# Two self attentions fused with the projection and layer norm ahead of them, and a first expert whose rows are picked by a one-hot product, in a two-layer perceiver block

## What is computed

```python
x = x + L0_xattn(layernorm(x), ctx)   # cross attention, projection+norm, self attention, projection+norm, MLP
x = x + L0_attn(layernorm(x))
x = x + L0_ffn(layernorm(x))          # 32 experts
x = x + L1_xattn(layernorm(x), ctx)   # cross attention, projection
x = x + L1_attn(layernorm(x))         # causal self attention, 16 heads of 16
x = x + L1_ffn(layernorm(x))          # 8 experts, below
# L1_ffn: each expert takes its 65 best tokens of each batch
scores = softmax(x @ router_w.T); gate, idx = top_k(scores.T, 65)
h = gelu(x[idx] @ w1 + b1); y = (h @ w2 + b2) * gate; out[idx] += y
```

## Time and profile before

| what | us |
|---|---|
| three timed runs, median (lowest to highest) | 1703.92 (1701.82 to 1704.51) |
| the profiled execution, its own time | 1701.66 |
| its span, first to last instruction | 1699.4 |
| TensorE busy | 1609.7 (95%) |
| VectorE busy | 1138.1 (67%) |
| ScalarE busy | 862.2 (51%) |
| GpSimd busy | 286.4 (17%) |
| layer 0: projection, norm and self attention | 660.9 to 732.3 |
| layer 1: projection, norm and causal self attention | 1519.7 to 1586.1 |
| last experts | 1598.1 to 1699.4 |

### The profile page before, as it was taken

One profiled execution on the slowest core, in us unless ns is written; L12 is line 12 of the kernel. 1 busy time (PEld: TensorE's weight loads), 2 busy tenths in 40 slices (PEclk: granted clock), 3 DMA queues, 4 the chain that ended last, 5 costly groups with the idle time before them and its releaser, 6 DMA issues. The chain is left out here.

```text
span 1699.4 us, 36130 instructions
## 1 busy us (share of the span) xinstructions
PE 1609.7 (95%) x12499; PEld 972.8 (57%) x12499; DVE 1138.1 (67%) x2012; ACT 862.2 (51%) x1784; POOL 286.4 (17%) x372
## 2 busy tenths in 40 slices
PE   7999999999999998999989999889999999989697
PEld 4444444454544544675867999635445454445497
DVE  5777788888888884747553111288888888855621
ACT  2222216777777775642532111257777777765332
POOL 1422220000000001020202444130000000000063
PEclk9999999999999999999989999989999999999899
DMA  6568756434434324400038999754343443304075
GB/s 194 180 201 219 205 165 137 75 57 65 65 56 69 60 38 127 67 2 1 1 112 274 325 314 320 238 85 66 57 74 56 66 64 56 56 1 102 13 220 141
DMA packets 150585, 196.29 MB, mean 116 GB/s; under 512 B 30394, under 2 KB 123805, under 8 KB 144465
## 3 DMA queue, kind: packets, MB, share of 16 engines
q1 hardware_dynamic: 141704, 188.83, 45.3%
q0 software_dynamic: 6720, 4.31, 1.5%
q10 hardware_dynamic: 2064, 1.87, 0.3%
HBM read 156.49 MB, written 41.39 MB: 116 GB/s over the span
## 5 line engine op out<-in xcount | busy, mean ns | idle before, releaser
L1187 ACT ACTIVATE probs<-ps 128x512 f32<-128x512 f32 x1024 | 558.5, 599 | 179.1 <-PE ps L1090 166.6
L1213 DVE TENSOR_REDUCE top<-ps 128x1 f32<-128x1024 f32 x504 | 594.1, 1220 | 60.1 <-PE ps L1069 47.1
L1090 PE MATMUL ps<-qst,kst 105*128 105x256 bf16 x2048 | 354.2, 276 | 6.8 <-DVE qst L1218 1.5
L1069 PE MATMUL ps<-kst,qst 105*128 105x512 bf16 x1008 | 306.3, 387 | 5.2 <-DVE top L1213 3.6
L1090 PEld LDWEIGHTS ps<-qst,kst 105*128 105x128 bf16 x2048 | 170.3, 100 | 227.5 <-ACT probs L1187 86.3
L1104 PE MATMUL ps_o<-probs,vst 128*32 128x256 f32 x4096 | 274.1, 385 | 2.3 <-ACT probs L1187 2.3
L1104 PEld LDWEIGHTS ps_o<-probs,vst 128*32 128x32 f32 x4096 | 106.8, 109 | 113.4 <-issue 50.9
L383 POOL COPY vst<-vall 128x512 f32 (+1 forms) x64 | 39.2, 613 | 697.0 <-PE ps_o L1104 694.3
L2312 PE MATMUL ps_h<-xe,vall 128*128 128x80 f32 x1024 | 149.6, 265 | 0.0
L2312 PEld LDWEIGHTS ps_h<-xe,vall 128*128 128x128 f32 x1024 | 136.4, 191 | 0.1
L1069 PEld LDWEIGHTS ps<-kst,qst 105*128 105x128 bf16 x1008 | 88.7, 98 | 62.9 <-issue 29.2
(11 more groups left out here) (439 smaller groups left out, 2008.8 us busy)
## 6 DMA issues: line engine op xcount, KB each, us to landing
kst<-kd SPq DMA_DIRECT2D x372, 128.0 KB
kd<-probs SPq DMA_DIRECT2D x64, 384.0 KB, 2.8
vall<-in_L_ffn_wg_dram SPq DMA_DIRECT2D x32, 512.0 KB, 6.3
vall<-in_L_ffn_wu_dram SPq DMA_DIRECT2D x32, 512.0 KB, 7.9
vall<-in_L_ffn_wd_dram SPq DMA_DIRECT2D x32, 512.0 KB, 5.9
w<-in_L_ffn_w_dram SPq DMA_DIRECT2D x16, 1024.0 KB, 7.4
vd<-square_weights SPq DMA_DIRECT2D x16, 512.0 KB, 4.1
vall<-vd SPq DMA_DIRECT2D x16, 512.0 KB, 6.3
```

The lines of the kernel that those rows point to most:

```text
L1069: mm = pe.matmul(ps1[:, slot1(m, u), x * 512:(x + 1) * 512], qst[:, m, qt * P:(qt + 1) * P], kst[:, m, c * W1 + x * 512:c * W1 + (x + 1) * ...
L1090: mm = pe.matmul(ps2[:, SCORES2[u], x, :], kst[:, m, kt * P:(kt + 1) * P], qst[:, m, :], start=True, stop=True)
L1187: nc.scalar.activation(probs[:, u % SLOTS, :, :], ps2[:, SCORES2[u], :, :], ACT.Exp).then_inc(probs_ready, 1)
L1213: v.tensor_reduce(top[:, b, qt, c:c + 1], ps1[:, slot1(m, u), :], AX, ALU.max).then_inc(mx, 1)
```

## The change

`normalize_and_attend` takes the place of `project_and_normalize` and `self_attention` where one followed the other (twice). It is one block: keys and queries of group 0 are made, copied and used by batch. The norm block behind the causal attention stays as it was. SyncE issues both sets of loads at the start of the fused block. In `experts1` the first expert's rows are picked from `xn` in SBUF by a product with a one-hot matrix, `first_hot`; gathers are left for the experts 1 to 7. The second part of the tables and the biases are moved into `up(0)`, the biases to other PSUM banks, the wait for the base ahead of `down(0)`, `turn_x(1)` behind `down(0)`. There are 45 filler matmuls in four places instead of 16 in one, and Gelu's table is loaded early. The core of the diff:

```diff
-def self_attention(pr, xT, query, key, value, causal, ahead=lambda sp: None):
+def normalize_and_attend(pr, src_tile, K, weight, bias, residual, total, query, key, value, causal, gain=None, shift=None,
+                         ahead=lambda sp: None, ahead_of_units=lambda sp: None):
...
+    FIRST_OF = {0: 1, 2: 2, 8: 3}
...
                 ahead(sp)
 
+                ahead_of_units(sp)
...
-                keys(0)
-                queries(0)
+                turn_src(0)
+                turn_src(1)
+                stay_busy(ps_f, 3)
+                for t in range(NT):
+                    project(t)
+                    if t + 2 < NT:
+                        turn_src(t + 2)
+                for t in range(QT):
+                    stay_busy(ps_t[:, 0, :], 3)
+                    turn_normed(t)
+                stay_busy(ps_t[:, 0, :], 2)
+                pe.wait_ge(x_copied, 1)
+                keys(0, 0, S)
+                queries(0, 0, S)
+                for t in range(QT, NT):
+                    turn_normed(t)
+                stay_busy(ps_p[:, 2, :], 2)
                 scores(0)
+                pe.wait_ge(x_copied, 2)
+                keys(0, S, N)
+                queries(0, S, N)
                 scores(1)
                 values()
                 keys(1)
...
-                copy_k(0)
+                copy_k(0, 0, slice(0, S))
+                copy_x(1)
                 exps(0, 0)
                 exps(0, 1)
-                copy_k(1)
+                copy_k(0, 1, slice(S, N))
+                copy_k(1, 2)
...
-                copy_q(0)
+                copy_q(0, 0, slice(0, S))
                 maxima(0)
+                copy_q(0, 1, slice(S, N))
                 maxima(1)
                 copy_v()
-                copy_q(1)
+                copy_q(1, 2)
...
-                for e in range(XB1):
+                pool.wait_ge(slots_ready, 1)
+                for e in range(1, XB1):
...
+                def first_x():
+                    pe.wait_ge(first_ready, 1)
+                    for b in range(B):
+                        for c in range(C):
+                            for t in range(b * QT, (b + 1) * QT):
+                                mm = pe.matmul(ps_x[:, c, b * CAP:(b + 1) * CAP], xn[:, t, c * P:(c + 1) * P],
+                                               first_hot[:, t, :], start=(t == b * QT), stop=(t == b * QT + QT - 1))
+                    mm.then_inc(x_turned, 1)
...
                 mm.then_inc(sc_t, 1)
+                stay_busy(38)
                 pe.wait_ge(taken_ready, 1)
...
                 mm.then_inc(taken_t, 1)
+                stay_busy(2)
                 pe.wait_ge(chosen_ready, 1)
...
                 mm.then_inc(placed, 1)
+                stay_busy(3)
+                first_x()
                 table(0)
...
+                stay_busy_in(ps_h[:, NH - 1, :], 2)
                 for e in range(E1):
                     for f in range(FT1):
                         up(e, f)
-                        if f == TURN_Y_AT and e:
-                            turn_y(e - 1)
-                        if f == TURN_X_AT and e + 1 < E1:
-                            turn_x(e + 1)
+                        if e == 0:
+                            if f == TABLE_AT:
+                                table(1)
+                            if f == BIAS_AT:
+                                bias()
+                        else:
+                            if f == TURN_Y_AT:
+                                turn_y(e - 1)
+                            if f == TURN_X_AT and e + 1 < E1:
+                                turn_x(e + 1)
                     down(e)
+                    if e == 0:
+                        turn_x(1)
...
+                nc.scalar.activation(first_gelu[:, :], pr.cf("parity")[:, 0:1], ACT.Gelu)
                 copy_x(0)
...
+                v.tensor_tensor(first_hot[:, :, :], bc(pr.cf("iota")[:, 1:CAP + 1], 1, NT), bc(slot[:, :, 0], 2, CAP),
+                                ALU.is_equal).then_inc(first_ready, 1)
...
-                v.tensor_tensor(base[:, :, :], acc, residual[:, :, :], ALU.add).then_inc(base_ready, 1)
+                v.tensor_tensor(base[:, 0:QT, :], ps_b[:, :, :], residual[:, 0:QT, :], ALU.add)
+                v.tensor_tensor(base[:, QT:NT, :], ps_y_rows, residual[:, QT:NT, :], ALU.add).then_inc(base_ready, 1)
```

More of the change, by code:

```diff
@@ L1316, in self_attention @@
             "summed", "o_copied", "o_turned", "inverted", "o_done"))
+        srcT = pr.sb(st, "srcT", [P, NT, K * P])
+        added = residual if bias is None else pr.sb(st, "added", [P, NT, D])
+        centred = pr.sb(st, "centred", [P, NT, D])
+        stats = pr.sb(st, "stats", [P, NT, 6])
+        mv = pr.sb(st, "mv", [P, NT, 2])
+        std = pr.sb(st, "std", [P, NT])
+        rstd = pr.sb(st, "rstd", [P, NT])
+        first_root = pr.sb(st, "first_root", [P, 1])
+        ps_p = ps_s.rearrange("p n j k -> p (n j) k")
+        ps_x = ps_of.rearrange("p x (c n) -> p x c n", c=C)
+        src_turned, copied, made, bias_added, steps, var_ready, std_ready, done, x_turned = (pr.sem(st, n) for n in (
+            "src_turned", "copied", "made", "bias_added", "steps", "var_ready", "std_ready", "done", "x_turned"))
+        x_copied = pr.sem(st, "x_copied")
         with nc.Block() as block:
@@ L1330, in _, with turn_src, project, stay_busy @@
             def _(pe):
[L1331 removed]
+                def turn_src(t):
+                    if t >= 2:
+                        pe.wait_ge(copied, t - 1)
+                    for c in range(K):
+                        mm = pe.transpose(ps_t[:, t % 2, c * P:(c + 1) * P], src_tile(t, c), pr.cf("ident"))
+                    mm.then_inc(src_turned, 1)
+                def project(t):
+                    pe.wait_ge(copied, t + 1)
+                    for c in range(K):
+                        mm = pe.matmul(ps_p[:, t, 0:D], srcT[:, t, c * P:(c + 1) * P], weight[:, c, :],
+                                       start=(c == 0), stop=(c == K - 1))
+                    mm.then_inc(made, 1)
+                def stay_busy(bank, n):
+                    for _ in range(n):
+                        pe.matmul(bank, pr.cb("identb"), pr.constsb[:, 0:512], start=True, stop=True)
+                def turn_normed(t):
+                    pe.wait_ge(done, t + 1)
+                    for c in range(C):
+                        mm = pe.transpose(ps_x[:, t // 2, c, (t % 2) * P:(t % 2 + 1) * P], dst[:, t, c * P:(c + 1) * P],
+                                          pr.cf("ident"))
+                    mm.then_inc(x_turned, 1)
+                def keys(c, first=0, end=N):
                     for x in range(C):
[L1333 removed]
+                        mm = pe.matmul(ps_kq[c][0][:, first:end], wk[:, x, c * P:(c + 1) * P], xT[:, x, first:end],
                                        start=(x == 0), stop=(x == C - 1))
                     mm.then_inc(k_made, 1)
[L1337 removed]
+                def queries(c, first=0, end=N):
                     for x in range(C):
[L1339 removed]
+                        mm = pe.matmul(ps_kq[c][1][:, first:end], wq[:, x, c * P:(c + 1) * P], xT[:, x, first:end],
                                        start=(x == 0), stop=(x == C - 1))
```

144 lines of the change are left out of this document (98 added, 46 removed).

## The result

The changed kernel takes 1696.17 us in the median of seven runs (1695.65 to 1699.26), the kernel before 1703.92 in seven (1701.82 to 1705.72). The ratio is 0.996, 95% interval 0.9951 to 0.997. The medians differ by 7.75 us; the ratio alone makes it 6.8 (5.1 to 8.3). The forecast was 1695.3 (1692.0 to 1699.5), faster with a chance of 0.89. The profiled execution of the changed kernel took 1695.69 us with a span of 1693.7. That is 5.97 less than the profiled execution before, where the sum of the prediction was 8.6.

The account below looks back on a forecast made before the run. TensorE, busy 95% of the span, was taken as the bound, so gains lie where it waits or runs at 1.2 GHz. 2.8 + 3.4 + 2.4 = 8.6 us off 1703.92 gave 1695.3 (own range 1692.6 to 1698.2).

Parts of the forecast that it names:

- Layer 0: First fused attention: first turn of the loop at 685.8 instead of 688.66, saving 2.8 us (2.8 to 4.0).
- Layer 1: Second fused attention: first turn of the loop at 1542.8 instead of 1546.25, saving 3.4 us.
- Cost nothing: Fused blocks: GpSimd's clearing of the value tile and SyncE's loads, moved along, add no time.
- The sign that it gave: Stage behind a fused block: waits behind the moved loads would show as TensorE idle at its start; none expected.
- The last block: Marks to second expert: early first `up`, partly given back, second expert at 1628.9 instead of 1631.32; saves 2.4 us (1.4 to 3.3).
- `down(0)` 3.58: Last block: the first expert's down product takes 3.58 us, ending at 1628.0.
- the gap ahead of `down(0)`: Last block: TensorE waits near 0.9 us for VectorE to add the base.
- Checked and not binding: Last block: second one-hot ready by 1620.3, expert 1's gathers have until 1628, expert 2's weights in time; no cost.
- From expert 1 on the cadence is TensorE's: Last block: from expert 1 on TensorE sets the pace as before, and the tail is the same.
- B: Rival, both fused blocks: ScalarE 1.4 us later behind the table load, by a drain; costs 2.2 us, 1697.5; 6%.
- C: Rival: stretches shorter, but new waits or 1.2 GHz elsewhere leave half; saving 3.6 to 5, 1699 to 1700.3; 18%.
- E: Rival, last block: the 38 fillers don't raise the clock; 9.2 us slower, 1713.1; 4%.

Follow-up runs that it names:

- e1: Changed kernel with the last expert block (`experts1`) of before, so both fused attentions alone: 1698.13 us, ratio 0.9969 to the kernel before.
- e6: Changed kernel with 33 instead of 38 fillers ahead of the marks' transposes: 1696.89 us, ratio 0.9929 to the kernel before.
- e12: Changed kernel without the early Gelu on ScalarE, so Gelu's table is loaded again behind the first expert's row copy: 1697.18 us, ratio 0.9965.
- e2: Kernel before with the new `experts1`, norm and attention blocks as before: 1702.14 us, ratio 0.9993 to the kernel before.
- e4: Changed kernel with biases behind table(0) in place of two fillers, and the base added ahead of the second table's slots: 1695.06 us, ratio 0.9952.
- e5: Changed kernel with five filler matmuls on TensorE ahead of `down(0)`: 1696.65 us, ratio 0.9933 to the kernel before.
- e8: e4 with 33 fillers instead of 38: 1695.07 us, ratio 0.9918 to the kernel before.
- e9: e4 with three experts in the first table instead of two: 1694.01 us, ratio 0.9944 to the kernel before.
- e11: e9 with GpSimd's wait for the base's store moved behind the gather of expert 4: 1693.78 us, ratio 0.995.

## Why the prediction was right or wrong

**The number** was right: 1696.17 against 1695.3, inside the range. The attentions did what the prediction said; in the last block the 2.4 of the sum were 0.1. That the number came so near in spite of this is in part luck. In the first pair of profiles the steps that were changed save 1.98 + 3.22 + 0.1 = 5.3 us, which would have given 1698.6, outside the forecast's own range to 1698.2. The other 2.4 of the 7.75 come from none of these steps. A part may be the stretch at 1.2 GHz that the old block of layer 1 shows in two of three profiles, 1.1 on the mean; the rest has no place that the traces show.

**Layer 0: right up to the first turn.** 2.8 forecast, 2.62 measured, in all ten profiles of the fused block by batch. TensorE's order came as worked out, and the scores cost all of the 1.16 that the bounds allowed. The path is 0.24 longer than forecast, 15.15 instead of 14.91: 0.18 stands ahead of the scores of pair 1, mostly keys and queries of batch 1, 1.93 instead of 1.75. ScalarE's second key copy wasn't the limit; it ended 7.78 us behind xT's start (7.71 forecast). Of the 2.62, 0.64 was lost again behind the block.

**Layer 1: right as to the mechanism, too small as to the size.** 3.4 forecast, 3.22 measured against the earlier trace rows. Against the other two profiles of the old block it is 4.86. The mean over the three, 4.3, together with layer 0's 1.98 makes 6.3, and e1, the attentions alone, measured 5.3 with an interval from 3.2 to 7.3. The step that was missed: a wait of 1.6 us on TensorE costs what it lasts and, in some executions, 1.6 us more behind it at 1.2 GHz. The change took away both.

**"Cost nothing": wrong in one place.** The clearing of the value tile and the loads of SyncE cost nothing that the traces show. But the prediction had no term for the semaphores that the longer block clears at its own end. The sign that it gave, TensorE idle at the start of the next stage, is there: 1.38 us instead of 0.74 in layer 0. In layer 1 the next stage starts as before, with a gap of 0.50 in both.

**The last block: the sum failed at "`down(0)` 3.58".** The steps up to it were good within 0.6 us in all: the first `up` came 5.4 us behind the marks instead of 4.8. The fillers took 10.5 us from the first to the marks' turn, as forecast (the clock rose 4.8 us behind the first; 2.9 to 6.7 was given), and that turn stood 1.07 behind the marks instead of 0.9. `first_x` took 2.00 instead of 1.7, the biases 1.12 (1.1), the base 1.29 (1.3), the gap ahead of `down(0)` was 0.80 (0.9). Then the clock fell, which put 1.7 us on `down(0)`: 5.47 instead of the 3.58 of the sum. So the second expert came 18.3 us behind the marks and not 16.0. The prediction had this gap, and had read in the earlier trace rows that the clock needs time to rise, but it priced the gap at its length alone. In five profiles with a gap of 0.80 there the clock fell four times (changed kernel twice, e6, e12; not in e2); in five without it (e4, e5, e8, e9, e11) never. e5, which differs in nothing but five fillers, ties the fall to the gap, as far as one profile can. What the fall costs is 1.5 to 1.7 us.

**"Checked and not binding", the gathers: wrong.** "From expert 1 on the cadence is TensorE's" holds from `down(1)` on: 7.90 us from one `down` to the next in every profile, 7.60 to the last. But the gather of expert 2, which waits for the second table's slots, came 1.01 us late in e2, 0.37 in e5, 0.30 in e11, 0.29 in e4 and 0.26 in e6. I had given a bound to the gathers of expert 1 and none to those of expert 2. It shows only where the second expert starts early, so it takes back part of what each repair brings.

**The rivals.** B did not happen: in layer 0's fused block the load ends at 677.70, and the exponentials start at 678.24, behind VectorE's first maximum. The load of a table is followed by the next instruction after 0.01 us in e12, and no drain like the one that the Trainium skill (ScalarE: Activation LUTs, "What ACT_TABLE_LOAD costs") adds is to be seen; the row was the better guide. C happened in part: a stretch at 1.2 GHz fell elsewhere, in `down(0)`. The 5.3 us of the changed steps are a little above C's 3.6 to 5. E's condition did not arise: the clock rose 4.8 us behind the first filler.

**What stays open.** Why the kernel before took 1709.13 us on one chip and 1703.4 to 1703.9 in the three other sets of runs, while the changed kernel took 1696.2 and 1697.0: the gain is 7.8 us on one and 12.1 on the other. No profile of the kernel before from that chip exists. The stretch between the two fused blocks, unchanged but for the 0.64 us, took anything from 827.9 to 832.1 us in fourteen profiles, and the path into the first xT 9.4 to 11.5, with the clock's stretches in other places each time. From the first turn of layer 1 to the marks it was 65.7 us in five of the profiles with a fused block and 67.1 in six, again by one stretch at 1.2 GHz more. Such differences are in the scatter of the medians and belong to no part of the change; the 1.8 us that the first pair of profiles shows there are of this kind.

## What to carry to other kernels

Start the half of the data that is ready instead of waiting for the whole: here that gave all of the gain that can be told from nothing, and the removed end of a block gave none that the median shows. A longer block also has more to clear up at its end: look at what the next one waits for first. When a start is moved forward, follow each thing that was hidden ahead of it (tables, biases, base, later gathers) to its new consumer, because it becomes the next wait: 5.5 us at the first `up` were 0.1 at the second expert, until the biases were moved too. And price an idle gap of TensorE by what the clock did behind such gaps in several profiles, since a single profile may not show what such a gap costs.

## What was not expected of the hardware

Idleness of 0.80 us in a busy stretch went, four times in five, with a stretch of about 3.4 us at 1.2 GHz. In the changed kernel this began 0.4 us behind the end of the gap. In e12 it began 0.4 before the end, when TensorE had been idle for 0.4 us (its window from 1617 to 1618 has a granted clock of 0.82, and the gap ends at 1618.06). The same code can fall on either side: the old attention block of layer 1 had its stretch at 1.2 GHz in two of three profiles and not in the one that was read first. And one chip took 5.2 us more than that of the first runs for the kernel before, but only 0.9 more for the changed one.
